# Two heads of attention in the two halves of TensorE's rows, and scores in a two-bank and a one-bank slot

## The chip, the cores and the metric

One core of a Trainium2 chip runs the whole program as one launch. The metric is the device time in microseconds (us). Engines: TensorE (PE; its weight loads are listed as PEld), VectorE (DVE), ScalarE (ACT), GpSimd (POOL) and SyncE (SP), which here only issues DMAs.

## What is computed

Two transformer layers over x of 4 x 1024 x 128 in float32. Cut to what matters:

```python
xn = layernorm(x)
x = x + attn0(xn) + fp4_ffn(xn)         # 16 heads of 8, causal over 1024 keys
xn = layernorm(x)
x = x + attn1(xn) + experts(xn)         # keys: a stride-3 convolution, 342 of them

scores = einsum('bhqd,bhkd->bhqk', q, k) * 8 ** -0.5   # masked: key after query
out = einsum('bhqk,bhkd->bhqd', softmax(scores), v)
# experts: 8 experts, the 2 best per row, plus a shared one
```

## The kernel before, in words

The stages follow each other, with a barrier of all engines between them: `first_projection`, `quantised_ffn`, `attention` for layer 0, `between_layers`, `attention` for layer 1, `experts`.

**Operands.** q and k of a head (8 numbers per row) are cut into three bf16 parts, and their products are summed as 48 rows (`PROWS`). `load_operands` (L193) fetches them for a group of 4 heads: `qp[g]` has 99 partitions (`KROWS + PARTS`), the even head of a pair in rows 0 to 47, the odd head in rows 48 to 95, the other 48 rows of each head at zero, and 3 rows for the maxima; `kp[g]` holds both heads of a pair, one under the other, with ones in the last 3 rows. The zeros are written by ScalarE during the FFN (`clear`, L659), and SP waits for them before it loads (L573). A load is 12 DMAs. The groups of layer 1's first batch are loaded by SP during `between_layers` (group 0, L1294), at the start of `attention` (group 1, L941) and after the first maxima (groups 2 and 3, L960).

**A unit** is one batch element and one group of 4 heads; there are 16 in each layer. For a unit PE computes

- *fills* (L1034 to L1051): scores with queries on the partitions, up to 512 columns in one of three PSUM banks (`BANKS`) used in turn. Where the diagonal is crossed, a matmul with the identity adds a mask (L1044). DVE takes the row maximum of each bank (L1153). In layer 0 there are 38 fills per unit, 16 of them leading ones without a mask; in layer 1 there are 17.
- the *tail*: DVE cuts the negated maxima into three bf16 parts (L1165 to L1173), PE turns them (`turn_max`, L1056), DVE copies them (L1180), and SP stores them with one DMA into the last 3 rows of `qp` (L957).
- *pairs* (L1077): two matmuls of 99 rows with keys on the partitions, one for each head, into the two banks of `p_st[half]`; the maxima's rows subtract the maximum. ScalarE takes the exponential (L1129), POOL zeroes what is unseen (L993) in one of a ring of four buffers (`RING`).
- *weighings* (L1096): probabilities times v in f32, four heads in four groups of 32 columns of the array. A unit has 12 in layer 0 and 5 in layer 1.
- `turn_out` (L1065): the sums, copied by ScalarE (L1138), are turned by four f32 transposes into a bank of the same three, and DVE scales them (L1187, L1191). Two per unit.

**What sets the order.** `Geometry.order` (L758) is a planner that runs in Python when the program is built. It simulates the engines with constants (L58) and writes one list, in which fills of unit n+1, turns, pairs and weighings of unit n are interleaved by readiness and priority. Every engine walks through this list in order. A fill, `turn_max` and `turn_out` each take the next bank; `fresh_bank` (L1028) waits for the use three before.

**Other users.** In layer 0 POOL also cuts the expert weights (L925). In layer 1 it sends rows to the experts' slots (L1005). In `between_layers` SP stores the parts of q and k chunk by chunk (`store_q1`, `store_k1`), and ScalarE waits for the store of a chunk before it overwrites the buffer two chunks later (L1429). In `experts`, DVE casts the first rows (`stage_x`, L1906, called at L1988) before PE's first matmul (L1735), and POOL adds the bias `bo` (L1714) at the start.

## Time and profile before

| | us |
|---|---|
| median of 3 runs | 1249.71 (1248.92 to 1250.62) |
| profiled execution, its own time | 1255.12 |
| its span, first to last instruction | 1253.2 |
| first projection and FFN | to 188.7 |
| attention, layer 0 | 188.7 to about 675 |
| between the layers | to 778.9 |
| attention, layer 1 | 778.9 to 1014 |
| experts | from 1016.8 |

The profile is of one execution. Busy time of PE has modelled ends: matmuls overlap, so its steady rate is better read from starts than from durations. In a timeline merged instructions show as xN with the time from the first start to the last end. Idle time before a group is given with the event that ended it.

### The profile page before, as it was taken

The page shows a single profiled execution, that of the slowest core. Times are in us where ns is not written, and L with a number is a line of the kernel's source. Part 1 is how long each engine was busy: PE and PEld are TensorE (multiplying, and loading weights), DVE is VectorE, ACT ScalarE, POOL GpSimd, SP SyncE. Part 2 cuts the span into 40 slices and gives each one's busy share as a digit, 9 for nine tenths or more (in the row PEclk, how much of TensorE's full clock was granted, in tenths as well). Part 3 has the DMA queues.
Part 4 walks back from the last instruction along what each step waited for, and adds up shares of the span by engine and source line. Part 5 has one row for each costly group of instructions (what it writes and reads, how often), then busy time and mean ns, then how long its engine had stood idle before and what let it go on. Part 6 is the DMA issues. An engine that isn't in the chain of part 4 may idle for free. (4 is left out here: it accounts for less than half of the span.)

```text
span 1253.2 us, 22218 instructions
## 1 busy us (share of the span) xinstructions
PE 1124.7 (90%) x7518; PEld 617.1 (49%) x7518; DVE 943.8 (75%) x2098; ACT 736.4 (59%) x1148; POOL 448.7 (36%) x714
## 2 busy tenths in 40 slices
PE   4668878999999999999998785799998969999997
PEld 2336662343434444444442563344444438888874
DVE  7979979788888888888881563677776646777776
ACT  3567540666666666666667343366666647777762
POOL 6002220232323323322222110366676661566640
PEclk9888996999999999999999796699999989999999
DMA  4322790013202121211000022222222252677543
GB/s 135 101 76 68 112 118 18 2 37 110 85 27 87 53 92 43 87 51 62 27 1 2 9 72 68 61 65 57 65 65 54 72 176 92 188 243 244 175 112 90
DMA packets 94975, 103.52 MB, mean 83 GB/s; under 512 B 17217, under 2 KB 72838, under 8 KB 94864
## 3 DMA queue, kind: packets, MB, share of 16 engines
q1 hardware_dynamic: 88928, 93.09, 27.6%
q0 software_dynamic: 4992, 8.48, 2.0%
q8 instruction: 61, 1.00, 0.3%
q10 hardware_dynamic: 944, 0.54, 0.2%
q14 instruction: 50, 0.41, 0.1%
HBM read 64.67 MB, written 38.43 MB: 82 GB/s over the span
## 5 line engine op out<-in xcount | busy, mean ns | idle before, releaser
L1129 ACT ACTIVATE a_probs<-a_pst 128x1024 f32<-128x1024 f32 (+4 forms) x544 | 413.8, 812 | 283.9 <-PE a_pst L1077 282.5
L1153 DVE TENSOR_REDUCE a_tops<-a_ps 128x1 f32<-128x512 f32 (+9 forms) x624 | 342.3, 591 | 95.0 <-PE a_ps L1047 80.9
L993 POOL TENSOR_SCALAR_AFFINE_SELECT a_probs<-a_probs 128x256 f32<-128x256 f32 (+3 forms) x384 | 180.4, 482 | 386.5 <-ACT a_probs L1129 382.1
L1047 PE MATMUL a_ps<-kp,qp 96*128 96x512 bf16 (+9 forms) x1280 | 293.1, 307 | 0.8 <-DVE a_tops L1153 0.6
L1077 PE MATMUL a_pst<-qp,kp 99*128 99x512 bf16 (+4 forms) x1088 | 259.5, 331 | 14.3 <-DMA qp<-a_top_rows 10.5
L1096 PE MATMUL a_po<-a_probs,vh 128*32 128x512 f32 (+4 forms) x2176 | 231.9, 499 | 2.6 <-POOL a_probs L993 2.5
L1153 DVE TENSOR_REDUCE a_tops_lead<-a_ps 128x1 f32<-128x512 f32 x256 | 161.8, 683 | 5.7 <-PE a_ps L1047 5.5
L1044 PE MATMUL a_ps<-mask_s,identb 128*128 128x128 bf16 (+8 forms) x624 | 144.5, 234 | 13.3 <-DMA kp<-k_parts 6.0
L1047 PEld LDWEIGHTS a_ps<-kp,qp 96*128 96x128 bf16 x1280 | 112.0, 101 | 79.1 <-DVE a_tops_lead L1153 15.4
L1077 PEld LDWEIGHTS a_pst<-qp,kp 99*128 99x128 bf16 (+1 forms) x1088 | 91.8, 99 | 110.1 <-ACT a_probs L1129 43.5
L1044 PEld LDWEIGHTS a_ps<-mask_s,identb 128*128 128x128 bf16 x624 | 59.5, 99 | 132.6 <-DVE a_tops L1153 62.1
L1722 POOL DMA_INDIRECT chosen_rows<-e_slot_y,e_slot_x x92 | 92.8, 1009 | 85.6 <-DVE e_slot_y L1944 43.8
L1932 DVE TENSOR_TENSOR e_tails<-e_hidden,e_heads 128x512 fp32r<-128x512 f32 x124 | 87.1, 703 | 33.1 <-ACT e_heads L1866 29.4
L1096 PEld LDWEIGHTS a_po<-a_probs,vh 128*32 128x32 f32 (+1 forms) x2176 | 43.3, 108 | 71.3 <-issue 61.5
L1859 ACT ACTIVATE e_hidden<-e_pup,e_slot_b 128x512 f32<-128x512 f32 x92 | 63.2, 688 | 24.1 <-PE e_pup L1737 19.2
L1005 POOL DMA_INDIRECT slot_rows<-rows,slots x64 | 63.3, 990 | 14.0 <-issue 11.5
L151 POOL TENSOR_TENSOR f_hq<-f_v,f_sc 128x704 f32<-128x704 f32 x16 | 22.8, 1424 | 119.6 <-DVE f_v L711 112.1
L1187 DVE RECIPROCAL a_inv_sum<-a_ps 128x16 f32<-128x16 f32 x64 | 16.4, 256 | 62.2 <-PE a_ps L1065 58.9
L1065 PE MATMUL a_ps<-ident,a_o_raw 128*128 128x128 f32 x256 | 41.5, 285 | 3.5 <-ACT a_o_raw L1138 1.9
L1138 ACT ACTIVATE a_o_raw<-a_po 128x512 f32<-128x512 f32 x64 | 38.3, 598 | 10.3 <-PE a_po L1096 10.3
L1930 DVE CAST e_heads<-e_hidden 128x512 fp32r<-128x512 f32 x62 | 27.8, 448 | 20.2 <-ACT e_hidden L1859 14.0
L597 PE MATMUL f_pg<-wg,big 128*128 128x352 f32 x64 | 27.4, 512 | 16.9 <-DVE f_h L692 15.9
(294 smaller groups left out, 1636.9 us busy)
## 6 DMA issues: line engine op xcount, KB each, us to landing
e_slot_w<-weight_parts SPq DMA_DIRECT2D x23, 1024.0 KB
weight_parts<-a_cut SPq DMA_DIRECT2D x18, 512.0 KB, 3.0
qp<-q_parts SPq DMA_DIRECT2D x64, 96.0 KB
slot_rows<-empty_row SPq DMA_DIRECT2D x4, 1495.0 KB, 28.6
e_slot_x<-slot_rows SPq DMA_DIRECT2D x23, 260.0 KB
a_raw<-in_wraw SPq DMA_DIRECT2D x18, 256.0 KB, 3.6
qp<-q_parts SPq DMA_DIRECT2D x64, 64.0 KB
q_parts<-o SPq DMA_DIRECT2D x24, 128.0 KB
```

The costliest lines, as they stand in the source:

```text
L993: pool.affine_select(out=seen, in_=seen, compare_op=ALU.is_ge, fill=0.0, base=m0, pattern=[[0, 2], [1, mw]], channel_multiplier=-1 if laye ...
L1005: pool.indirect_dma_start(dram["slots"], bass.IndirectOffsetOnAxis(sb["slots"][:, choice, t:t + 1], 0), sb["rows"][:, t, :], None, bounds_ ...
L1044: pe.matmul(out, sb["identb"][:, :], mask_s[r][:, 0:mw].unsqueeze(1).broadcast_to([P, nh, mw]), start=True, stop=False, skip_group_check=True)
L1047: last = pe.matmul(bank[:, i * room:i * room + w], sb["qp"][slot][0:KROWS, j, f["qt"] * P:(f["qt"] + 1) * P], sb["kp"][slot][0:KROWS, j // ...
L1065: last = pe.transpose(turned[:, t * P:(t + 1) * P], o_raw[:, t * P:(t + 1) * P], sb["ident"][:, :])
L1077: last = pe.matmul(p_st[half][0:st["rows"], i, off:CHUNK], sb["kp"][slot][0:KROWS + PARTS, half, st["kt"] * P:st["kt"] * P + st["rows"]], ...
L1096: last = pe.matmul(p_o[VW * j:VW * (j + 1), st["off"]:CHUNK], sb["vh"][n % 2][0:st["rows"], st["kt"], j, :], probs[local % RING][0:st["row ...
L1129: act.activation(probs[local % RING][0:st["rows"], 2 * part:2 * part + 2, st["off"]:CHUNK], p_st[part][0:st["rows"], :, st["off"]:CHUNK], ...
L1153: dve.tensor_reduce(out, scores, AX.X, ALU.max).then_inc(s["banks_read"], 1)
L1722: pool.indirect_dma_start(dram["chosen"], bass.IndirectOffsetOnAxis(slot_x[r % XR][:, t, E:E + 1].bitcast(U32), 0), slot_y[r % YR][:, t, : ...
L1859: act.activation(hidden[m % RR][:, :], p_up[m % UR][:, :], ACT.Gelu, bias=biases(j)[:, k:k + 1])\
L1932: dve.tensor_tensor(tails[m % HR][:, :], hidden[m % RR][:, :], heads[m % HR][:, :].bitcast(F32), ALU.subtract)\
```

## The change

Each head of a pair gets its own half of the 128 rows: the even head rows 0 to 47 and the maxima's parts rows 48 to 50, the odd head rows 64 to 111 and 112 to 114. `qp` becomes 128 x 2 pairs x T, so nothing has to be cleared. A *couple* is a fill of both heads of a pair (or of both pairs, up to 256 columns). Scores go to a slot of two banks (both heads at once) and a slot of one bank in turn; a couple whose turn is the one-bank slot is done in two halves, one head at a time. The planner's prices change with it (`TWO_AT_ONCE`).

```diff
-KROWS = 2 * PROWS
+ROWS_HALF = P // 2
-BANKS = 3
+SLOTS_OF_BANKS = 2
+BOTH, TWO_AT_ONCE = 2, 1.25
-def load_operands(sp, sb, dram, layer, keys, b, g):
+def load_operands(sp, sb, dram, layer, keys, b, g, halves=range(2)):
-    for odd in range(2):
-        r0 = PROWS * odd
+    for odd in halves:
+        r0 = ROWS_HALF * odd
-            sp.dma_start(sb["qp"][g][rows, odd:GH:2, 0:T], src).then_inc(loaded, 16)
+            sp.dma_start(sb["qp"][g][rows, :, 0:T], src).then_inc(loaded, 16)
...
-        p_s = [... psum_tensor(f"a{layer}_ps{i}", [P, 512], F32) for i in range(BANKS)]
+        p_s = [... psum_tensor(f"a{layer}_ps{i}", [P, 2 - i, 512], F32) for i in range(SLOTS_OF_BANKS)]
```

In the planner's loop, where a fill is taken:

```diff
+                if opened is not None and (mine or taken == C):
+                    f, which, opened = opened, 1, None
+                elif mine:
+                    f, which, opened, taken = taken, 0, taken, taken + 1
+                else:
+                    f, which, taken = taken, BOTH, taken + 1
+                pe = start + ((TWO_AT_ONCE if which == BOTH else 1) * (each_pe[f] + mask_pe[f]))
```

PE's fill. The mask takes two matmuls for each head, since a half of the rows holds only half of the identity (`swapped` is a copy of the constants with the halves exchanged, made by two DMAs):

```diff
+                odds = ((0, 0), (1, 1)) if part == BOTH else ((part, 0),)
                 if f["mask"]:
-                    pe.matmul(out, sb["identb"][:, :], mask_s[r][:, 0:mw]..., start=True, stop=False)
+                    for i in range(2):
+                        for odd, where in odds:
+                            rows = slice(ROWS_HALF * odd, ROWS_HALF * (odd + 1))
+                            pe.matmul(out, sb["idents"][i][rows, :], masks[i][r][rows, 0:mw]..., start=i == 0, stop=False)
-                for i, j in enumerate(f["heads"]):
-                    last = pe.matmul(bank[:, i * room:i * room + w], qp[0:KROWS, j, ...], kp[0:KROWS, j // 2, ...])
+                for i, a in enumerate(f["pairs"]):
+                    for odd, where in odds:
+                        rows = slice(ROWS_HALF * odd, ROWS_HALF * odd + PROWS)
+                        last = pe.matmul(banks[:, where, i * room:i * room + w], qp[rows, a, ...], kp[rows, a, ...])
```

Pairs and maxima:

```diff
                 for i in range(2):
+                    rows = slice(ROWS_HALF * i, ROWS_HALF * i + PROWS + PARTS)
-                                     kp[0:KROWS + PARTS, half, ...], qp[0:KROWS + PARTS, 2 * half + i, ...]
+                                     kp[rows, half, ...], qp[rows, half, ...]
...
-                    sp.dma_start(sb["qp"][n % GROUPS][KROWS:KROWS + PARTS, :, :]..., top_rows[:, :])
+                    for odd in range(2):
+                        r0 = ROWS_HALF * odd + PROWS
+                        sp.dma_start(sb["qp"][n % GROUPS][r0:r0 + PARTS, :, :]..., top_rows[odd * each:(odd + 1) * each, :])
```

DVE reduces both banks of a couple with one instruction. The rest moves work: the eight `clear` passes and SP's waits for them go; in `between_layers` the loads of groups 0 and 1 are issued in four halves of 6 DMAs, one each after the stores of chunks 3, 4, 5 and 6 (before: all 12 of group 0 after chunk 3, group 1 in the next stage); POOL adds the bias in units 1 to 8 of layer 1's attention; DVE stages the first rows of the experts in unit 8:

```diff
+                if what == "end" and layer == 1 and k == 0 and 1 <= n <= CHUNKS:
+                    add_bias(n - 1)
...
+                if what == "end" and layer == 1 and k == 0 and n == B * GROUPS // 2:
+                    stage_first_rows()
...
-            stage_x(0)
             run(step)
```

The memsets of ones in `kp` cover all 128 partitions (before: 3), and PE waits once, at the start of layer 0's attention, for the constants' copies and the experts' empty rows.

## Rows read from the trace of the kernel before

**Rows 1.** The page, busy time of the engines over the span.
```profile
PE 1124.7 (90%) x7518; PEld 617.1 (49%) x7518; DVE 943.8 (75%) x2098; ACT 736.4 (59%) x1148; POOL 448.7 (36%) x714
```
**Rows 2.** Busy time by stretch: first unit, steady part of layer 0, of layer 1.
```profile
core 0: us, PE busy (x) PEld busy (x) DVE busy (x) ACT busy (x) POOL busy (x), PEclk, DMA share, GB/s
188.70:217.00 28.30, 25.37 (x94) 8.15 (x94) 27.39 (x53) 1.28 (x1) 0.73 (x2) 0.63 0.03 8
217.00:660.00 443.00, 440.18 (x3272) 179.20 (x3273) 371.93 (x704) 282.12 (x385) 132.12 (x286) 0.99 0.17 55
...
820.00:990.00 170.00, 158.64 (x1492) 78.64 (x1492) 127.14 (x324) 105.73 (x151) 115.90 (x178) 1.00 0.24 60
```
**Rows 3.** Groups by form, of 260 to 600 us, then of 830 to 980 us.
```profile
L1153 DVE TENSOR_REDUCE a_tops_lead<-a_ps 128x1 f32<-128x512 f32 x185 | 117.0, 683 | 3.3 <-PE a_ps L1047 3.0
...
L1138 ACT ACTIVATE a_o_raw<-a_po 128x512 f32<-128x512 f32 x22 | 13.0, 593 | 0.0
```
**Rows 4.** Timeline, PE: start us, us, engine line op out<-in xcount.
```profile
655.16 0.60 PE L1077 MATMUL a_pst<-qp,kp 99*128 99x512 bf16 x2
655.59 0.38 PE L1047 MATMUL a_ps<-kp,qp 96*128 96x512 bf16 x1
655.90 1.07 PE L1096 MATMUL a_po<-a_probs,vh 128*32 128x512 f32 x8
656.90 0.23 PE L1044 MATMUL a_ps<-mask_s,identb 128*128 128x128 bf16 x1
661.30 0.40 PE L1077 MATMUL a_pst<-qp,kp 99*128 99x128 bf16 x4
745.36 1.03 PE L1326 MATMUL b_pq<-big,wq 128*128 128x512 f32 x2
1002.88 0.66 PE L1065 MATMUL a_ps<-ident,a_o_raw 128*128 128x128 f32 x4
```
**Rows 5.** Timeline, DVE, in the first unit of layer 0.
```profile
195.45 0.68 DVE L1153 TENSOR_REDUCE a_tops_lead<-a_ps 128x1 f32<-128x512 f32 x1
198.46 2.48 DVE L1153 TENSOR_REDUCE a_tops_lead<-a_ps 128x1 f32<-128x512 f32 x4
204.44 1.94 DVE L1153 TENSOR_REDUCE a_tops<-a_ps 128x1 f32<-128x384 f32 x4
```
**Rows 6.** The maxima's store: durations in ns; waits of 260 to 600, of 830 to 980.
```profile
L957 SPq DMA_DIRECT2D qp<-a_top_rows x32: 723/748/794, 214.2 to 996.5; - x32
...
PEld a_pst L1077 <- DMA qp<-a_top_rows: 4.5, 11, 0.6
...
PEld a_pst L1077 <- DMA qp<-a_top_rows: 7.4, 11, 0.7
```
**Rows 7.** Timeline between the layers and at the start of layer 1's attention.
```profile
745.16 0.78 SPq L201 DMA_DIRECT2D qp<-q_parts  x1
...
753.87 7.30 SPq L190 DMA_DIRECT2D q_parts<-q_kept  x6
...
758.26 0.60 ACT L1430 ACTIVATE q_kept<-b_pq 128x512 bf16<-128x512 f32 x1 [12.15 <-DMA q_parts<-q_kept]
...
792.63 0.33 PE L1044 MATMUL a_ps<-mask_s,identb 128*128 128x172 bf16 x1 [5.97 <-DMA kp<-k_parts]
```
**Rows 8.** Start of the experts: timeline; by line, min/median/max ns, first and last start.
```profile
1018.34 1.63 DVE L1914 TENSOR_TENSOR e_xt<-big,e_xh 128x512 fp32r<-128x512 f32 x1
...
L1912 DVE CAST e_xh<-big x8: 419/421/1533, 1016.8 to 1219.5; 128x512 fp32r<-128x512 f32 x8
...
L1716 POOL TENSOR_TENSOR x<-x,bo x8: 1261/1448/1726, 1016.8 to 1026.6; 128x512 f32<-128x512 f32 x8
```
**Rows 9.** FFN: the clearing; busy times with it (92:124) and without (124:156).
```profile
L660 ACT ACTIVATE qp<-identb 96x2048 bf16<-96x2048 bf16 x8 | 15.2, 1901 | 0.0
...
92.00:124.00 32.00, 25.74 (x125) 19.29 (x126) 30.72 (x54) 23.25 (x41) 6.94 (x5) 0.89 0.22 62
124.00:156.00 32.00, 26.79 (x148) 20.66 (x148) 30.72 (x55) 18.65 (x48) 8.32 (x6) 1.00 0.74 112
```

More of the change, by code:

```diff
@@ L727, in __init__ @@
         self.key_tiles = -(-self.keys // P)
-        self.fills, self.steps = [], []
+        self.couples, self.steps = [], []
         for qt in range(T // P):
@@ L732, in __init__ @@
                 if lead:
-                    for j in range(GH):
-                        self.fills.append(dict(heads=[j], qt=qt, k0=0, width=CHUNK, mask=None, partial=True))
+                    for a in range(GH // 2):
+                        self.couples.append(dict(pairs=[a], qt=qt, k0=0, width=CHUNK, mask=None, partial=True))
                 mask_w, mask_r = P, 0
@@ L738, in __init__ @@
                 mask_w, mask_r = width - P * qt // STRIDE, P * qt % STRIDE
-            per = 4 if width <= 128 else 2 if width <= 256 else 1
-            for j in range(0, GH, per):
-                self.fills.append(dict(heads=list(range(j, j + per)), qt=qt, k0=lead, width=width,
-                                       mask=(mask_r, mask_w), partial=False))
+            per = 2 if width <= 256 else 1
+            for a in range(0, GH // 2, per):
+                self.couples.append(dict(pairs=list(range(a, a + per)), qt=qt, k0=lead, width=width,
+                                         mask=(mask_r, mask_w), partial=False))
         for c in range(T // CHUNK):
@@ L769, in order @@
         steps_share = share([2 * p + w for p, w in zip(pair_pe, weigh_pe)])
-        fills_share = share(fill_dve)
         order, pe, dve, act, pool, use = [], 0, 0, 0, 0, 0
-        banks, score_banks, exp_end = [0] * BANKS, [0, 0], {}
+        slot, slots, held, score_banks, exp_end = 0, [0] * SLOTS_OF_BANKS, [None] * SLOTS_OF_BANKS, [0, 0], {}
         split_end, maxima_end, sums_end, copied_end, loaded = {}, {}, {}, {}, dict.fromkeys(range(GROUPS), 0)
-        pairs = fills = sums = 0
+        pairs = sums = filled = taken = halves = 0
+        opened = None
         turns, outs, emptied, sums_free, before = [], [], [], 0, None
@@ L778, in order @@
             at = n + steps_share[k]
-            bank = max(pe, banks[use % BANKS] + PASS_US)
+            bank = max(pe, slots[slot] + PASS_US)
             ready = []
@@ L790, in order @@
                               + (0 if before == "weigh" else PASS_US), 4, "weigh"))
-            m, f = fills // F, fills % F
-            if m < units and m in loaded and m < n + 2 and not (turns and f == F - 1) and (m < 2 or m - 2 in split_end):
-                behind = m + fills_share[f] < at + 1 + AHEAD[self.layer]
+            m = filled
+            if m < units and m in loaded and m < n + 2 and not (turns and halves >= 2 * C - 2) \
+                    and (m < 2 or m - 2 in split_end):
+                behind = m + halves / (2 * C) < at + 1 + AHEAD[self.layer]
                 ready.append((max(bank, loaded[m]), 2 if behind else 5, "fill"))
@@ L945, in _ @@
             use = 0
-            for what, n, k, part in order:
+            for what, n, k, part, slot, before in order:
                 if what == "end" and layer == 0 and n < (B - 1) * GROUPS:
@@ L1027, in _, with fresh_bank @@
         def _(pe):
-            def fresh_bank(use):
-                if use >= BANKS:
-                    pe.wait_ge(s["banks_read"], read(use - BANKS))
-                return p_s[use % BANKS]
-            def fill(n, k, use):
-                f, slot = geo.fills[k], n % GROUPS
-                if k == 0:
-                    pe.wait_ge(sb["loaded"][slot], 16 * LOADS * (layer * B + n // GROUPS + 1))
-                bank, w, nh = fresh_bank(use), f["width"], len(f["heads"])
+            def fresh_bank(slot, before):
+                if before is not None:
+                    pe.wait_ge(s["banks_read"], read(before))
+                return p_s[slot]
@@ L1039, in fill @@
+            def fill(n, k, part, slot, before):
+                f, at = geo.couples[k], n % GROUPS
+                if n // GROUPS not in started[at]:
+                    started[at].add(n // GROUPS)
+                    pe.wait_ge(sb["loaded"][at], 16 * LOADS * (layer * B + n // GROUPS + 1))
+                banks, w, nh = fresh_bank(slot, before), f["width"], len(f["pairs"])
                 room = 512 // nh
+                odds = ((0, 0), (1, 1)) if part == BOTH else ((part, 0),)
                 if f["mask"]:
@@ new lines, in fill @@
+                for i, a in enumerate(f["pairs"]):
+                    for odd, where in odds:
+                        rows = slice(ROWS_HALF * odd, ROWS_HALF * odd + PROWS)
+                        last = pe.matmul(banks[:, where, i * room:i * room + w],
+                                         sb["qp"][at][rows, a, f["qt"] * P:(f["qt"] + 1) * P],
+                                         sb["kp"][at][rows, a, f["k0"]:f["k0"] + w],
+                                         start=not f["mask"], stop=True, skip_group_check=True)
@@ L1100, in weigh @@
                 last.then_inc(s["pv_done"], 1)
-            use = 0
-            for what, n, k, part in order:
+            started = [set() for _ in range(GROUPS)]
+            if layer == 0:
+                pe.wait_ge(sb["later_in"], 16 * (sb["later_loads"] + 4))
+            for what, n, k, part, slot, before in order:
                 if what == "fill":
-                    fill(n, k, use)
+                    fill(n, k, part, slot, before)
                 if what == "pair":
@@ L1118, in _ @@
             use, last_out = 0, None
-            for what, n, k, part in order:
+            for what, n, k, part, slot, before in order:
                 if what == "turn_out":
@@ L1283, in _ @@
         def _(sp):
+            halves = iter([(g, odd) for g in range(2) for odd in range(2)])
             for b in range(B):
```

244 lines of the change are left out of this document (131 added, 113 removed).

## The prediction

> **What bounds the kernel now.** I read the page's busy times first: TensorE (PE) is busy for 90% of the span and VectorE (DVE) for 75% [rows 1]. The stretches come next [rows 2]. In attention 0's steady part (217 to 660 us) PE is busy 440.2 of 443 us at a granted clock of 0.99, DVE 371.9, ScalarE 282.1; in attention 1 (820 to 990) PE 158.6 of 170 us at 1.00, DVE 127.1, ScalarE 105.7, POOL 115.9. So both stages hang on PE. A busy PE includes modelled ends, so I turn to the rate. By the groups of 260 to 600 us, 185 leading reductions (16 for each unit of 4 heads) are 11.56 units, 29.4 us each; in 830 to 980 us, 22 copies of the sums (2 per unit) are 11 units, 13.6 us each [rows 3].
>
> **What a piece costs on PE** [rows 4]. Two bf16 matmuls of 512 columns take 0.60 us and one 0.38, so a column stream of 512 costs about 0.215 us (2.4 GHz); a 512-column f32 matmul fills 1.03 us alone, and a weighing, four of them in four column groups, 1.07. Less the 0.22 us in which the last drains, 0.85. The fill at 655.59 is followed by the weighing 0.31 us later, 0.1 over its stream, and the next work (656.90) comes 1.00 us after that, 0.15 over: a change between forms costs 0.10 to 0.15 us.
> A unit of attention 0 then streams: fills 18432 columns, 7.68 us; masks 4096, 1.71; pairs 18432, 7.68; weighings 4608 columns at four passes, 7.68; turns of the sums, 8 at 0.11 (0.66 less 0.22 for four, the row at 1002.88), 0.88. Sum 25.6; the other 3.8 of 29.4 us are changes of form and waits. Attention 1, with 43 to 342 keys and some 0.05 us as the least for a short matmul (four of 128 columns take 0.40): fills 2.85, masks 1.06, pairs 3.2, weighings 3.2, turns 0.88: 11.2 of 13.6, other 2.4.
>
> **What a piece costs on DVE** [rows 5]. Four reductions of 512 take 2.48 us and one 0.68: one per 0.60, so 0.533 of data and 0.065 fixed; four of 384 take 1.94, one per 0.46, the same fixed part. A unit of attention 0 reads 18432 columns, 19.2 us, in 38 reductions, 2.5, and spends some 2.7 on the split, the turned maxima and the scaling: 24.4, 83% of 29.4. DVE is the next bound.
>
> **The change, part by part.**
> *Pairs.* The two heads sit in rows 0 to 63 and 64 to 127 and write different banks. The trace has no two row groups at once. Bounds: together they take from 1.0 of one (as the four column groups, [rows 4]) to 2.0 (serial). I take 1.1, since the column groups are the nearest row. Attention 0: 7.68 becomes 4.22; attention 1: 3.2 becomes 1.76.
> *Fills.* Slots alternate, and three turns per unit take one too, so two couples of three go whole into the two-bank slot and the third as two halves through the one-bank slot, with no partner. The factor is 2/3 x 0.55 + 1/3 = 0.70: 7.68 becomes 5.38, and 2.85 becomes 2.0.
> *Masks.* Half the rows carry half the identity, so each head's mask takes two matmuls. Whole couples stream as much as before x 1.1, halves double: 1.71 becomes 2.39. In attention 1 there are 40 short ones for 17 at about 0.05 us: 1.06 becomes 1.9.
> PE's streams, attention 0: 25.6 becomes 20.6. Attention 1: 11.2 becomes 9.7.
> *Maxima in two stores.* SP issues a second DMA, 0.75 us each now [rows 6]; PE's first pair waits for the last and has the fills queued behind it. That store already ends eleven idle times of the weight loads in 260 to 600 us (4.5 us in all) and eleven in 830 to 980 (7.4), so it is not covered. The second should land 0.6 us later (0 to 0.8): +0.6 per unit, and SP's next loads slip as much.
> *Form changes.* Turns of maxima and sums were in the same full form as the fills and no longer are: 3 per unit, some 0.1 each way: +0.3 (0 to 0.6).
> PE then needs 20.6+3.8+0.9 = 25.3 us per unit, and 9.7+2.4+0.9 = 13.0.
> *DVE.* 27 reductions for 38: 24.4 becomes 23.6; attention 1 (13 for 17) 10.2 becomes 9.9.
> *The slots.* Three banks let PE run 1.2 us ahead of DVE; two slots only one read, 1.13 us or 0.60 in turn. While a half is read for 0.60 us PE must fill two banks, about 0.5 us to the reduction (mask 0.11, stream 0.215, drain some 0.2, [rows 4]), and a weighing of 1.0 us in between leaves DVE empty. PE at 25.3 and DVE at 23.6 could run at 25.3 or, if the pairs cost 1.0, at 24.6; I estimate 1.4 us lost per unit (0 to 3.3): 26.7. In attention 1, PE 13.0, DVE 9.9: +0.2, 13.2.
> Attention 0: 15 steady units x (29.4-26.7) = -40 us. Attention 1: 15 x 0.4 = -6. First units only fill, at half clock (0.63 in 188.7 to 217, [rows 2]): two banks take 0.4 longer there, +1 us per stage, +2 together.
> *Loads in halves* [rows 7]. From 745.16 SP issues 12 loads until 753.87; the store of the next chunk's q stands behind them, and ScalarE waits 12.15 us for it. Six go first now: -4.3 at this wait, the next store is 3 earlier: -3 (0 to -4.5) at the stage's end. Chunk 7's store stands behind the last half, but attention 1's barrier is later.
> *Group 1 loaded early.* Attention 1's second unit waits 5.97 us for its operands, issued only behind chunk 7's stores: -6 (-4 to -6.5).
> *Early staging* [rows 8]. The cast (from 1016.8) and the remainder (to 1019.97) of the first rows stand before the first expert matmul: -3.2. They move to DVE in unit 8, 1.1 us, where it has slack. The bias goes to POOL in units 1 to 8, 1.45 each, queued before POOL's zeroing that weighings wait for; POOL has 54 us free in 170 and the ring of four covers it. POOL's adds no longer run beside DVE's first steps (cast 1.53 us against a median 0.42): about -1.8. Together -5.
> *Clearing gone.* Eight passes of 1.90 us leave ScalarE, but DVE is busy 30.72 of 32 us with them and without [rows 9]: 0. Loads and empty rows start earlier in a stage that waits for neither; memsets of kp cover more partitions but as many elements in each: 0 (they end long before kp is loaded). The two copies of the constants are small.
> Sum: -40-6+2-3-6-5 = -58. The profiled execution took 1255.1 us (span 1253.2), 5.4 over the median 1249.7; I take the difference from the median: **1192**.
>
> By the Trainium skill's "TensorE: Matmul & The Clock Gate", Part 3 (Packing small matmuls), four row tiles were measured at 3.07 times one, not 4; an estimate of 1.3 for two follows. No row here shows row groups. With 1.3 in place of 1.1, by the same sum, PE needs 1.5 us more per unit of attention 0 and 0.5 of attention 1, and the time would be some 1220.
>
> **Rivals.**
> *A: the row groups do not run at once.* Pairs and fills stay, all masks double. Attention 0 +1.7+0.9 = 2.6 a unit, attention 1 +1.3+0.9 = 2.2: +72-12 = 1310 us. Against it: column groups overlap fully. 5%.
> *B, slower: the clock.* PE streams 25.6/29.4 = 87% now at full clock, 20.6/26.7 = 77% then. The granted clock did fall in the first unit, where PE only fills for DVE [rows 2]. At half clock a unit costs 41.2+4.7 = 45.9 in attention 0 (+19) and 19.4+3.3 = 22.7 in attention 1 (+10): 435 us for all. It decides above 58/435 = 13% of the steady stretch; at 20% the time is 1279. For it: two heads at once leave PE idle. Against: in 124 to 156 us it stays 1.00 with PE busy 26.8 of 32, less by streams [rows 9]. 7%.
> *C: the slots cost more.* DVE empties behind each weighing: 28.6 and 13.8 per unit, -12+3, and -12 elsewhere: 1229. For: weighings of 1 us against reads of 0.6. 19%.
> *D: DVE is kept fed.* With pairs at 1.0 of one, 24.6 and 12.2: -72-21-12: 1145. For: the planner orders the work by these slots. 12%.
> Forecast 57%.
>
> **How the numbers follow.** About 0.2% can be told from no change. The forecast's own range is 1165 to 1218. Faster: forecast, C and D, less 2% of C's upper end for no change, 86%; same 2%; slower A and B, 12%. The range for 8 in 10 leaves out A and B above and half of D below, 18% in all: 1147 to 1240.
>
> **What would show it.** Right: the two pair matmuls of 512 in under 0.45 us; units at 26 to 27.5 and 12.7 to 13.7 us; DVE over 88% in attention 0 with reductions of 1024 at 1.2 us; 27 reductions per unit; the wait on the maxima 0.6 longer; no 12 us wait near 750, no 6 us wait in attention 1, the first expert matmul with the stage's start. Wrong: pair matmuls one after the other (A), a clock under 0.9 in the steady parts (B), DVE under 84% with waits on fills behind weighings (C).

## The result and the profile after

The changed kernel takes 1349.16 us in the median of 4 runs (1339.30 to 1351.88), where the kernel before took 1250.16 beside it: a ratio of 1.078 (1.072 to 1.084), slower by 7.8%. The prediction was 1192 us, in a range of 1147 to 1240, and gave "slower" a chance of 0.12. Both the sign and the range were wrong.

The profiled execution took 1339.3 us, its span is 1337.4. On the page TensorE is busy for less of a longer span [rows 1], and its clock, which was 0.99 and 1.00 in the steady parts of the kernel before [rows 2], is at 7 or 8 tenths in both attentions (at 5 and 6 where they start):
```profile
PE 1123.7 (84%) x8295; PEld 573.0 (43%) x8302; DVE 950.5 (71%) x1873; ACT 727.2 (54%) x1140; POOL 447.5 (33%) x714
...
PE   4658877888888888888897786878889889999997
...
PEclk9979985888877788888888896877877878999999
```
Now by stage. All stages below are cut at the first score matmul and the last turned sum. Busy times of the kernel before, attention 0 and attention 1 (columns as in [rows 2]):
```profile
188.80:691.60 502.80, 491.61 (x3568) 195.18 (x3568) 402.45 (x766) 304.61 (x417) 140.98 (x308) 0.97 0.15 49
778.90:1013.30 234.40, 212.07 (x1888) 102.37 (x1888) 162.19 (x414) 136.86 (x193) 148.17 (x228) 0.95 0.24 62
```
The same stages of the changed kernel, and two stretches inside attention 0, one after the other:
```profile
core 0: us, PE busy (x) PEld busy (x) DVE busy (x) ACT busy (x) POOL busy (x), PEclk, DMA share, GB/s
189.10:743.70 554.60, 477.29 (x3984) 163.22 (x3984) 399.38 (x591) 308.74 (x417) 141.95 (x308) 0.83 0.14 44
824.40:1102.60 278.20, 230.73 (x2256) 93.78 (x2256) 178.62 (x366) 137.19 (x193) 157.41 (x236) 0.78 0.19 51
...
551.80:562.00 10.20, 9.69 (x55) 3.59 (x57) 5.91 (x9) 4.02 (x5) 2.03 (x5) 0.50 0.23 66
562.00:585.90 23.90, 20.08 (x200) 6.90 (x196) 19.76 (x28) 15.19 (x21) 8.47 (x16) 1.00 0.22 73
```
Attention 0 is 51.8 us longer and attention 1 43.8; the start takes 0.3 more, and the rest is shorter: between the two 80.7 us for 87.3, from attention 1's end to the first expert matmul 3.6 for 6.8, the experts 231.2 for 233.1. That is the whole difference of the spans (1337.4 against 1253.2). The clock does not sink a little; it swings between its two levels, here 10 us at 1.2 GHz and 24 at 2.4, and the swing has the length of a unit (33.4 us on average; 6.8 to 13.7 us of each are at 1.2 GHz).

The timeline of the changed kernel shows what went as planned, and where a unit ends:
```profile
547.60 0.19 DVE L1196 TENSOR_TENSOR a_tops<-a_tops,a_tops_lead 128x16 f32<-128x16 f32 x1
...
548.44 1.30 POOL L940 TENSOR_TENSOR first_rows<-a_raw,first_rows 128x512 fp32r<-128x512 f32 x1
548.65 1.13 DVE L1205 CAST a_top_parts<-a_top_rest 128x32 bf16<-128x32 f32 x1
...
550.05 1.54 DVE L1186 TENSOR_REDUCE a_tops<-a_ps 128x2 f32<-128x256 f32 x2
550.61 0.23 PE L1081 MATMUL a_ps<-consts,a_top_parts 128*96 128x128 bf16 x1 [2.02 <-DVE a_tops L1186]
551.52 0.21 DVE L1214 COPY a_top_rows<-a_ps 96x128 bf16<-96x128 bf16 x1
551.74 1.05 PE L1090 MATMUL a_ps<-ident,a_o_raw 128*128 128x128 f32 x4 [0.90 <-DVE a_top_rows L1214]
...
565.71 0.41 PE L1103 MATMUL a_pst<-qp,kp 51*128 51x512 bf16 x2
...
566.86 0.38 PE L1103 MATMUL a_pst<-qp,kp 51*128 51x512 bf16 x2
```
At the full clock two pair matmuls of 512 columns now take 0.38 to 0.41 us, as one did, where the two took 0.60 [rows 4]. Rival A is out. At the unit's end PE stands still for 2.02 and 0.90 us. The turn of the maxima has to wait for a slot, and that slot's fill is read by a reduction which stands on DVE behind the five steps of the split; one of these, the cast, takes 1.13 us beside a POOL addition (0.18 where POOL does nothing). Then come the copy, the two stores (1.5 us of issue) and only then the next pairs. In the kernel before the planner left 2 to 2.5 steps of pairs to be done when the split began, with 8 or 9 pieces of work between the turn and the next unit's first pair; by the changed costs and slots it leaves 1 step and 4 pieces (the orders of the two kernels' planners, attention 0).

### The profile page after: what moved, and what is told of

It is laid out like the page before. It is cut to its first block and busy times, and to the rows that moved or that the text cites. A ratio compares the mean times of both kernels' runs of the same rounds, so it can differ in the third digit from the quotient of the medians.

```text
span 1337.4 us, 23579 instructions
## 1 busy us (share of the span) xinstructions
PE 1123.7 (84%) x8295; PEld 573.0 (43%) x8302; DVE 950.5 (71%) x1873; ACT 727.2 (54%) x1140; POOL 447.5 (33%) x714
## 5 line engine op out<-in xcount | busy, mean ns | idle before, releaser
L1186 DVE TENSOR_REDUCE a_tops<-a_ps 128x2 f32<-128x86 f32 (+14 forms) x466 | 331.6, 740 | 114.2 <-PE a_ps L1072 112.2
L1103 PE MATMUL a_pst<-qp,kp 51*128 51x512 bf16 (+4 forms) x1088 | 233.2, 386 | 37.4 <-DMA qp<-a_top_rows 25.1
L1072 PE MATMUL a_ps<-kp,qp 48*128 48x512 bf16 (+9 forms) x1280 | 250.0, 346 | 3.0 <-DVE a_tops L1186 2.7
L1186 DVE TENSOR_REDUCE a_tops_lead<-a_ps 128x1 f32<-128x512 f32 (+1 forms) x189 | 159.9, 872 | 42.6 <-PE a_ps L1072 41.8
L1066 PE MATMUL a_ps<-consts 64*128 64x256 bf16 (+4 forms) x704 | 116.0, 246 | 32.1 <-DVE a_tops L1186 15.6
L1066 PEld LDWEIGHTS a_ps<-consts 64*128 64x128 bf16 x704 | 48.0, 100 | 181.9 <-DVE a_tops L1186 94.8
L1103 PEld LDWEIGHTS a_pst<-qp,kp 51*128 51x128 bf16 (+1 forms) x1088 | 68.7, 102 | 122.4 <-ACT a_probs L1155 63.6
L1072 PEld LDWEIGHTS a_ps<-kp,qp 48*128 48x128 bf16 x1280 | 87.0, 108 | 77.1 <-DVE a_tops_lead L1186 45.1
L1066 PE MATMUL a_ps<-swapped 64*128 64x256 bf16 (+4 forms) x704 | 115.5, 245 | 0.0
L153 POOL TENSOR_TENSOR f_hq<-f_v,f_sc 128x704 f32<-128x704 f32 x16 | 22.7, 1421 | 119.4 <-DVE f_v L709 117.7
L1090 PE MATMUL a_ps<-ident,a_o_raw 128*128 128x128 f32 x256 | 47.6, 316 | 14.2 <-DVE a_top_rows L1214 11.5
L1066 PEld LDWEIGHTS a_ps<-swapped 64*128 64x128 bf16 x704 | 51.7, 107 | 14.5 <-issue 9.3
```

The lines of the kernel that those rows point to most:

```text
L1066: pe.matmul(out, sb["idents"][i][rows, :], masks[i][r][rows, 0:mw].unsqueeze(1).broadcast_to([ROWS_HALF, nh, mw]), start=i == 0, stop=Fals ...
L1072: last = pe.matmul(banks[:, where, i * room:i * room + w], sb["qp"][at][rows, a, f["qt"] * P:(f["qt"] + 1) * P], sb["kp"][at][rows, a, f[" ...
L1103: last = pe.matmul(p_st[half][0:st["rows"], i, off:CHUNK], sb["kp"][at][rows, half, st["kt"] * P:st["kt"] * P + st["rows"]], sb["qp"][at][ ...
L1186: dve.tensor_reduce(out, scores, AX.X, ALU.max).then_inc(s["banks_read"], 1)
```

## The experiments

A unit is timed from one turn of the maxima to the next. In the medians, each kernel is compared with runs of the kernel before on the same chip (1250.8 to 1251.6 us).

**The planner's constants.**
```diff
-    0.00042, 0.105, 0.07, 0.00104, 0.165, 0.17, 0.00083, 1.1, 2.2, 9.0)
+    0.00042, 0.105, 0.07, 0.00104, 0.165, 0.17, 0.00083, 3.0, 3.6, 9.0)
```


> The changed kernel with two constants of its planner set nearer to what its own trace shows: the split of the maxima 3.0 us for 1.1, their store 3.6 for 2.2. Nothing else differs but the order of the same work. Theory M (the chain of the maxima: the last fill of a unit, the split, the turn and the two stores stand between a unit's last pair and the next one's first, since the planner now leaves one step of pairs behind the split where it left 2 to 2.5 before; TensorE runs dry there and the clock falls because of it): with three steps left the wait of TensorE for the split maxima, 3.1 us per unit of attention 0, falls under 1, units of attention 0 go from 33.5 to 28 to 30 us, the granted clock there from 0.85 to over 0.93, and the time to 1250 to 1290 us. Theory K (the clock falls because two heads at once leave TensorE with less to stream, wherever the gaps lie): the clock stays under 0.88 and the time within 1 per cent of 1349. Theory S (two slots starve VectorE at each fill): units stay over 32 us.


1343.8 us, 1.074 (1.072 to 1.076). Busy times of e1, attention 0:
```profile
189.80:736.20 546.40, 493.97 (x3984) 171.10 (x3984) 393.43 (x590) 308.11 (x417) 141.86 (x308) 0.83 0.14 45
```
The gaps went: the stretch from the turn at 415.5 to that at 446.8 us has none over 0.6 us. Yet the clock is at 0.83 as before, and attention 0 gained 8 us. So the clock does not need the gaps; theory M as the sole cause fell here. Not one unit is free of half clock: those with 6.8 us of it take 31.2 to 31.9 us, those with 20.5 take 36.7.

**Filler where TensorE waits for the split.**
```diff
+                spare = fresh_bank(slot, before)
+                for _ in range(10):
+                    pe.matmul(spare[:, 0, :], sb["identb"][:, :], sb["kp"][n % GROUPS][:, 0, 0:CHUNK], start=True, stop=True)
                 pe.wait_ge(s["split_steps"], ...)
```


> The changed kernel with ten extra matmuls of 512 columns into the free slot before TensorE waits for the split maxima of a unit (their result is overwritten), 2.2 us of streams at full clock in a gap of 3.1. Theory K: the granted clock rises from 0.85 to over 0.93 in attention 0 and, since the units took 31.6 us in the stretches at full clock against 33.5 over all, the time falls by 20 to 35 us, to some 1320. Theory M: the clock may rise, but the chain stays: units stay over 31 us and the time within 1.5 per cent of 1349. If the clock stays where it is, the gap behind the turned maxima (their stores) is enough by itself to lower it.


1401.5 us, 1.117 (1.110 to 1.124). Attention 0 of e2:
```profile
189.00:769.90 580.90, 499.80 (x4144) 172.55 (x4144) 400.57 (x591) 307.51 (x417) 142.44 (x308) 0.88 0.13 42
```
Neither expectation was met. The filler needs the slot as well, so it ran behind the wait and not in it (a gap of 1.9 us stands ahead of it still), and it lengthened the chain. What it did show: ten full-height matmuls more in each unit, and the clock of attention 0 at 0.88 for 0.83, although the unit grew. More work and more height go together here, so this run does not tell them apart.

**Three slots of one bank again.**
```diff
-SLOTS_OF_BANKS = 2
+SLOTS_OF_BANKS = 3
...
+                    pe.matmul(out, sb["identb"][:, :], masks[0][r][:, 0:mw]..., start=True, stop=False, ...)
+                for i, (odd, a) in enumerate(f["heads"]):
+                    rows = slice(ROWS_HALF * odd, ROWS_HALF * odd + PROWS)
```


> The changed kernel with the scores in three slots of one bank again and the order of work, the masks and one head per bank as before; the pairs keep the two heads in two halves of the rows. Two reductions more in a unit of attention 0 and three more in attention 1 than before. Theory S: VectorE is fed as before, units of attention 0 fall to 26 to 28 us and of attention 1 to 13.3, time 1190 to 1230. Theory M: the planner leaves 1.5 steps behind the split (2 to 2.5 before, 1 in the changed kernel), so the wait for the maxima is in part still there: units 29 to 31, time 1250 to 1300. Theory K: TensorE has the least to stream of all versions, the clock stays under 0.88 and the time over 1300.


1407.1 us, 1.125 (1.122 to 1.127), slower than the changed kernel. Of the three expectations only theory K's (a clock under 0.88, over 1300 us) fits. TensorE's timeline in e3 shows a cause that none of them names:
```profile
405.18 0.23 PE L1053 MATMUL a_ps<-consts 128*128 128x128 bf16 x1
405.34 0.33 PE L1057 MATMUL a_ps<-kp,qp 48*128 48x384 bf16 x1
405.61 0.23 PE L1053 MATMUL a_ps<-consts 128*128 128x128 bf16 x1
405.77 0.33 PE L1057 MATMUL a_ps<-kp,qp 48*128 48x384 bf16 x1
```
The same in the kernel before:
```profile
657.19 0.22 PE L1044 MATMUL a_ps<-mask_s,identb 128*128 128x128 bf16 x1
657.25 0.38 PE L1047 MATMUL a_ps<-kp,qp 96*128 96x512 bf16 x1
```
A mask of 128 columns is followed by its fill after 0.16 us when the fill is in half height, after 0.06 when both are full: 0.10 us for the change. Back to full height costs as much (384 columns stream in 0.16, the next mask comes 0.27 later). Two units of e3 that stand one after the other:
```profile
454.90:492.50 37.60, 36.46 (x230) 10.65 (x227) 26.37 (x52) 19.55 (x26) 9.48 (x20) 0.77 0.14 50
492.50:524.00 31.50, 30.59 (x229) 9.76 (x225) 25.57 (x50) 19.24 (x26) 7.87 (x19) 0.95 0.15 43
```
The work is the same and TensorE has next to no gap in either; the clock alone makes 6.1 us. By these two, 1 us at half clock costs an estimated 0.45 us, and a unit wholly at 2.4 GHz would take some 30 (0.95 is 3.4 us at half clock: 31.5 less 1.5).

**Masks in halves too, three slots.**
```diff
-                    pe.matmul(out, sb["identb"][:, :], masks[0][r][:, 0:mw]...)
+                    for i in range(2):
+                        pe.matmul(out, sb["idents"][i][rows, :], masks[i][r][rows, 0:mw]..., start=i == 0, ...)
```


> The kernel of e3_one_bank (three slots of one bank, two heads of a pair in two halves of the rows) with the masks in halves of the rows too, as in the changed kernel: two matmuls of 64 rows for each. In e3_one_bank the units of attention 0 took 31.6 us with 3.4 us at half clock and 37.5 with 17.1, a line with 0.43 us per us at half clock and 30.2 at none. Theory F (a change between full height and half height costs TensorE 0.09 to 0.11 us: mask to fill 0.178 us there against 0.085 in the kernel before): with 40 changes per unit less and 1.7 us of masks more the line falls to 27 to 28.5 us at none, and the time to 1330 to 1370, since the clock still falls. Theory S (the two slots are what slows the changed kernel at full clock): the line falls below 27, and the time below 1300. If neither form nor slots matter it stays at 1407.


1288.8 us, 1.030 (1.028 to 1.033). Both stages of e5:
```profile
188.60:713.30 524.70, 472.75 (x3984) 170.34 (x3984) 413.46 (x798) 307.04 (x417) 142.42 (x308) 0.85 0.14 47
794.80:1056.90 262.10, 217.20 (x2256) 94.68 (x2256) 182.93 (x464) 135.19 (x193) 157.56 (x236) 0.84 0.19 54
```
118 us less than e3, with one edit, which takes out some 40 changes of height per unit: they were dear (theory F), though the time is below F's range and in S's. It is also 60 us under the changed kernel, which differs from it in slots and order alone, so theory S has its part, though at a low clock one cannot say how much of this the slots cost by themselves (e13 below can).

**Less for TensorE, all of it in full height.** The kernel of before without one of each pair's two matmuls from the second unit on; what it computes is then not the reference's.
```diff
-                for i in range(2):
+                for i in range(1 if n else 2):
```


> The kernel of before, all matmuls in full height and three slots, which leaves out the second head's matmul of each pair from the second unit of each attention on: its scores are whatever the bank held, and the output is not the reference's. TensorE streams 3.84 us less per unit of attention 0, 21.8 us; the other engines do the same work. Theory K (the granted clock follows how much TensorE streams): units cannot go under VectorE's 24.4, TensorE's share of streams falls from 87 to 80 per cent or less and the clock falls in part of each unit, so that units stay at 27 to 30 us in place of 26 to 26.5. Theory R (row halves or the gaps at the unit's ends lower the clock, and full-height work does not): the clock stays 1.0, units are 26 to 27 us and the time 1180 to 1200.


1214.6 us, 0.971 (0.968 to 0.974). Twelve units of attention 0 in e6:
```profile
275.20:608.10 332.90, 322.22 (x2368) 118.30 (x2369) 298.91 (x575) 225.26 (x310) 108.06 (x232) 1.00 0.21 69
```
The clock never left 2.4 GHz there, with streams of 21.8 in 27.7 us (79%, about the share that the prediction gave the changed kernel) and gaps of up to 1.5 us at the units' ends. Theory K, that such a share is enough to lower the clock, fell; the time, 1214.6, is above theory R's range. For taking 3.84 us of streams out of a unit shortened it by 1.9 (from 29.6 over the same twelve units), not by 3.8, in a kernel with nothing else changed. Waits of the weight loads (us in total, times, longest) over twelve units of the kernel before, then of e6:
```profile
PEld a_pst L1077 <- ACT a_probs L1129: 18.4, 51, 0.8
...
PEld a_pst L1077 <- ACT a_probs L1129: 32.9, 78, 0.8
```
The waits for ScalarE's exponentials grow by 1.2 us per unit; those of the fills' weight loads for DVE's reductions by 2.1 (53.6 to 78.4 us), with DVE busy for 298.9 of 332.9 us.

**The pair matmuls twice, in half height.**
```diff
-                for i in range(2):
+                for i in (0, 1, 0, 1):
```


> The changed kernel with each pair's two matmuls issued twice in turn (the same result again): TensorE streams 3.84 us more per unit of attention 0, as much as before the change, in half heights. Theory K by streams: the clock returns to over 0.95 in attention 0, units (33.3 us on average with 10.2 us at half clock, about 29 at full) take 31 to 33 us, and the time is no more than 1 per cent above 1349 or below it. Theory R (half-height work or gaps lower the clock): the clock stays at 0.85 to 0.88 and units grow by 3 to 5 us, the time to 1410 or more.


1395.1 us, 1.116 (1.113 to 1.119). Attention 0 of e7:
```profile
190.00:787.90 597.90, 539.21 (x4752) 209.73 (x4752) 401.61 (x591) 310.93 (x417) 142.10 (x308) 0.82 0.13 41
```
3.84 us of half-height streams more in each unit, and the clock stays down: theory R held in the clock, with the gaps of the changed kernel in place (its time is 15 us under R's range). The units grew to 36 us, so that streams are still a smaller share of them than in e6; this run alone does not rule the share out. With e1 (gaps gone, clock low) and e6 (gaps there, clock full) it points to the height of the matmuls, which the next run tests alone.

**All 64 rows of a half.** The rows added hold zeros on one side, so the columns and the result stay. Outside the attentions ScalarE zeroes `qp` again during the FFN, and each load has two small transfers more.
```diff
-                    rows = slice(ROWS_HALF * odd, ROWS_HALF * odd + PROWS)
+                    rows = slice(ROWS_HALF * odd, ROWS_HALF * (odd + 1))
...
+        sp.dma_start(sb["qp"][g][r0 + PROWS:r0 + PROWS + PARTS, :, :]..., sb["zeros"][...]).then_inc(loaded, 16)
```


> The kernel of e5_half_masks whose fills and pairs run over all 64 rows of their half in place of 48 and 51; the rows added hold zeros on one side (the rows of the maxima are zeroed with each load, two small transfers more), so the result is the same and the columns streamed are the same. Theory H (the granted clock falls because the array is used in less of its height: 48 or 51 rows of a half now, 96 and 99 of 128 before, while full-height work at 78 per cent of the time in e6_less_pairs kept 1.0): the clock of attention 0 rises from 0.87 to 0.9 or more, units from 31.4 to 29 to 30.5 us, the time from 1289 to 1255 to 1275. Theory G (rows do not matter; halves at once simply leave TensorE idle more often, or the gaps at the units' ends lower the clock): nothing changes, 1285 to 1295.


1274.5 us, 1.021 (1.018 to 1.025). Both stages of e8:
```profile
188.20:694.50 506.30, 457.08 (x3984) 168.01 (x3984) 413.52 (x798) 307.81 (x417) 141.92 (x308) 0.88 0.15 49
778.50:1035.80 257.30, 204.13 (x2256) 91.64 (x2256) 184.52 (x464) 135.34 (x193) 157.07 (x236) 0.90 0.21 56
```
Multiplying by zeros made the kernel 14 us faster than e5. In the profiled executions (e5's is its slowest, e8's its fastest) attention 0 took 506.3 for 524.7 at 0.88 for 0.85, attention 1 257.3 for 262.1 at 0.90 for 0.84. In the steady stretch from 260 to 660 us the clock is 0.90 for 0.87, and a unit takes 30.3 us for 31.4: theory H, at the upper end of its time. Theory G is out. The transfers of zeros are not free: the stage between the layers takes 84.0 us for 81.5.

**Padded, with the planner's constants.** e8 with the edit of e1.

> e8_padded with the planner's constants of e1_plan (split of the maxima 3.0 us, store 3.6), which leaves 2 to 2.5 steps of pairs behind the split for 1.5. In e5_half_masks TensorE is idle 2.96 us per unit of attention 0, 1.8 of it before the turned maxima in most units. Theory M: that gap goes, units 1 to 2 us shorter than in e8_padded, the time 15 to 35 us shorter. If the clock rules all, units stay as in e8_padded and the time within 8 us of it.


1274.8 us, 1.019 (1.017 to 1.021), no gain on e8 in the sum, but not in the stages:
```profile
190.10:681.40 491.30, 449.62 (x3984) 165.79 (x3984) 398.29 (x798) 305.34 (x417) 142.92 (x308) 0.96 0.15 51
765.40:1036.80 271.40, 219.47 (x2256) 93.78 (x2256) 172.78 (x464) 138.02 (x193) 158.01 (x236) 0.86 0.19 53
```
In attention 0 padding and a filled end of the unit together hold the clock: thirteen of the fourteen units after the first two run wholly at 2.4 GHz and take 29.0 to 29.5 us; the stage is 11.5 us shorter than before the change. Attention 1 lost 14 us by the same constants.

**Pairs alone in halves (e9), and no halves at all (e11), both with the planner's constants of e1.** e9 keeps three slots and puts fills and masks back in full height (its pairs have 51 rows, not 64):
```diff
-                    rows = slice(ROWS_HALF * odd, ROWS_HALF * odd + PROWS)
+                    rows = slice(0, ROWS_HALF + PROWS)
```


> Pairs alone in two halves of the rows; fills over rows 0 to 111 (the other head's rows zero) and masks in full height, three slots of one bank, up to four heads in one, the other parts of the change kept, planner constants as in e1_plan. TensorE streams 3.84 us less per unit of attention 0 than e4_rest, and changes height at 20 to 35 places per unit for 0.1 us each. Theory F: the changes take 2 to 3.8 us back, units 28.5 to 30 us at full clock; theory H: with fills and masks in full height the clock is over 0.95. Together 1215 to 1240 us, against 1237 for e4_rest. If the clock falls below 0.92 here too, a half-height part of 3.8 us per unit is enough for it, and the time is 1240 to 1280.

e11 is e4 (below: all in full height, the other parts of the change kept) with the edit of e1.

> e4_rest (the kernel of before with the other parts of the change) with the planner's constants of e1_plan. Before, TensorE hardly waits at a unit's end (0.17 us idle per unit of attention 0, 0.9 of attention 1), so little is to be had: 1228 to 1240 us against 1237 for e4_rest; units of attention 1 that take 13.3 us may fall to 13.0.

e9: 1274.7 us, 1.018 (1.016 to 1.020). e11: 1267.3 us, 1.013 (1.011 to 1.015). Stages of e9:
```profile
188.40:703.30 514.90, 482.51 (x3568) 154.48 (x3568) 393.69 (x767) 306.76 (x417) 142.24 (x308) 0.98 0.15 48
787.60:1039.40 251.80, 218.68 (x1888) 93.19 (x1888) 163.52 (x417) 138.09 (x193) 157.88 (x236) 0.91 0.20 57
```
Stages of e11:
```profile
189.50:700.20 510.70, 495.18 (x3568) 193.05 (x3568) 399.95 (x766) 307.48 (x417) 142.68 (x308) 0.98 0.15 48
783.10:1030.70 247.60, 220.35 (x1888) 104.43 (x1888) 161.33 (x416) 137.94 (x193) 157.47 (x236) 0.95 0.20 57
```
Both missed their ranges, e11 by the constants: against e4 below, it has the same work and 8 us more in attention 0 and 22 in attention 1. That e9 missed for the same reason is argued, since it ran with these constants alone. An order that suits one layout is a bad one for another. At equal constants the steps read: pairs in halves, with the second store of the maxima (e11 to e9), cost 4.2 us in each attention, although they take 61 us of streams off attention 0, and the steady part of attention 0 stays at 2.4 GHz; fills and masks in halves as well, all padded (e9 to e10), gain 23.6 us in attention 0 and cost 19.6 in attention 1.

**The other parts of the change alone.** The kernel of before with the loads in halves, group 1 early, the bias and the first expert rows in attention 1.

> The kernel of before with the other parts of the change alone: attention 1's operands loaded in halves with group 1 early, the bias added and the first expert rows split in attention 1. By the terms of the prediction (3, 6 and 5 us) 1236 us, 1232 to 1242; all theories of attention expect the same, and granted clock 1.0 in both attentions as before. If it is not faster than before, those terms are wrong too.


1237.3 us, 0.989 (0.987 to 0.991), as expected. Stages of e4:
```profile
191.20:694.00 502.80, 490.46 (x3568) 194.85 (x3568) 402.58 (x766) 304.51 (x417) 140.74 (x308) 0.98 0.15 49
774.70:999.90 225.20, 211.40 (x1888) 102.33 (x1888) 161.51 (x416) 136.34 (x193) 158.50 (x236) 0.96 0.23 62
```

**Each attention in the form that suits it.** Attention 0 as in e10, attention 1 in full height as in e4.
```diff
+        tail_us, store_us = (3.0, 3.6) if self.layer == 0 else (TAIL_US, STORE_US)
...
+                    rows = slice(ROWS_HALF * odd, ROWS_HALF * (odd + 1)) if layer == 0 else slice(0, ROWS_HALF + PROWS)
```


> Attention 0 as in e10_padded_plan (two heads in padded halves of the rows, three slots of one bank, the planner's split 3.0 and store 3.6 us), attention 1 as in e4_rest (everything in full height, one store of the maxima, the old constants), the other parts of the change kept; what stays extra in attention 1 are the two small transfers of zeros with each load. Attention 0 took 491.3 us in e10_padded_plan against 502.8 in e4_rest, attention 1 225.2 in e4_rest: if the stages add up, the time is 1237 less 11, 1223 to 1230, below both kernels. If the stages do not add up (the clock of one stage carried into the next, the transfers of zeros in the way of loads) it is 1232 or more.


1229.2 us, 0.982 (0.981 to 0.984), below both kernels of this case. Stages of e12:
```profile
189.00:681.10 492.10, 450.82 (x3984) 165.92 (x3984) 397.30 (x798) 305.30 (x417) 142.36 (x308) 0.95 0.16 51
765.10:992.90 227.80, 211.60 (x1888) 101.80 (x1888) 161.43 (x416) 136.27 (x193) 158.24 (x236) 0.96 0.24 63
```
The stages add up within 3.4 us; attention 1's extra is small, and after its first fills and the unit behind them it runs at 2.4 GHz throughout, as before the change. Packing, in attention 0 alone and with new constants, gives some 8 us (1229.2 for e4's 1237.3).

**The changed kernel with both repairs**: the edits of e1 and e8 in it, its two slots kept.

> The changed kernel, two slots of two banks and one, with the two repairs that brought the three-slot version to 1275: all 64 rows of each half in fills and pairs, and the planner's split 3.0 and store 3.6 us. Theory H+M (height and the planner's constants are what the changed kernel lacks; the slots cost little): attention 0 goes from 554.6 us to 495 to 505 with the clock over 0.95, the time to 1270 to 1290. Theory S (the two slots cost 1 to 3 us per unit at full clock by themselves): units of attention 0 take 30.5 to 32 us where e10_padded_plan's took 29.0 to 29.2, TensorE and VectorE wait for one another in turn, the clock falls again in a part of each unit, and the time is 1295 to 1330.


1290.0 us, 1.031 (1.027 to 1.036). Both stages of e13:
```profile
190.70:696.10 505.40, 447.05 (x3984) 160.57 (x3984) 389.49 (x590) 305.70 (x417) 141.51 (x308) 0.94 0.15 49
780.70:1052.20 271.50, 214.58 (x2256) 89.16 (x2256) 175.59 (x366) 139.16 (x193) 157.59 (x236) 0.86 0.20 53
```
Units wholly at 2.4 GHz take 29.4 to 29.5 us, those of e10 mostly 29.0: two slots cost some 0.5 us per unit by themselves. Four of e13's units fell to half clock for a while, one of e10's did. So theory H+M holds for most of it, just past the slow end of its ranges for the stage and the clock.
Beside e1 this is the sharpest test of the height, for only the padding differs: the same slots, planner's constants and columns, and the same longest gap in a unit (0.6 us). The time falls by 54 us, attention 0 from 546.4 to 505.4 and its clock rises from 0.83 to 0.94; in e1 every unit is at half clock for a part, in e13 ten of fourteen for none. Those ten stream 20.6 us by the prediction's count in 29.4, a share of 70%, less than e6's 79, and hold 2.4 GHz. In attention 1 the two repairs together gain 6.7 us (278.2 to 271.5), and the clock stays at 0.86.

## Why the prediction was wrong

**The step that failed is the weight of rival B.** The prediction set the clock's fall at 7% and costed it at 1279. It named both sides: TensorE would stream less of the time, and in the stretch of 124 to 156 us the clock stays full with PE busy for less [rows 9]. The second argument decided, and it compared busy time alone; that stretch has six gaps, of 0.9 us at most, and matmuls of 96 and 128 rows. What the sum left out is that half-height matmuls do not hold the clock here as full-height ones do. With 48 and 51 rows in each half no unit of e1 stays at 2.4 GHz, with 64 in each half most of e13's do, with the same columns in the same order; e5 to e8 says the same with three slots. Nor does the share of streams by itself lower the clock, as the argument for rival B had it: 79% in e6 and 70% in e13's units hold it.
The decision point was right as far as it went. In the steady parts of the changed kernel the clock is 0.85 (248 to 683 us) and 0.80 (851 to 1085 us), so that 31 and 40% of them are at half clock, both far over 13%. With these shares and rival B's own units (26.7 and 45.9; 13.2 and 22.7) a unit comes to 31 and 15.9 us; measured are 33.4 and 16.7. By the prediction's sum that is an estimated 1297 us: the clock accounts for some 105 of the 157 us that the prediction missed. The rest is below.

**The unit at full clock was too short, 26.7 against 29.4 (e13).** The sum took every microsecond of streams saved as a microsecond gained, down to DVE's 24. e6 gives the measured exchange: 3.84 us fewer streams, 1.9 us shorter units, with more waits for ScalarE and for DVE. By this exchange the 5.0 us of streams saved (25.6 to 20.6) would have given an estimated 2.5. With the sum's own 0.9 for stores and changes and the slots' measured 0.5 (below) that is a unit of 28.3; the last 1.1 us of the 29.4 stays open. The terms beside it:
- Pairs at 1.1 of one: 1.0 in the trace, better than taken. The same holds for two fills of 512 in two halves (0.39 us for both).
- A change of form at 0.1 us: right (e3). In e9 units take 30.8 us, as in e11: some 25 new changes per unit between pairs and fills by the planner's order, an estimated 2.5 us, take most of the 3.84.
- Two slots at 1.4 us (0 to 3.3): 0.5 at full clock (e13 against e10). In the changed kernel, with the planner's constants and clock as they are, slots and order cost 60 us (e5). Rival C's mechanism, DVE left without a fill, is there in part (it waits for fills 6.5 us per unit, 2.5 before); the dearer place was the turn of the maxima, which waits for a slot whose fill is read behind the split. The prediction did not look there. Rival D had the pairs right at 1.0, but no packed version kept DVE fed: in e13's units at full clock it is busy for 83%.
- The second store at 0.6 us: PE's weight loads wait for the maxima's transfers 11.0 us in 12 units of attention 0, 0.9 each, where it was 0.4 [rows 6]: right. In attention 1 PE itself waits for them 14.7 us over 15 units for 6.7, and 4.5 of it are one wait (to 873.4), where both stores stand in SP's queue behind the loads of another group.
- That the planner would keep the units' ends covered was not weighed at all. It plans with a split of 1.1 us and a store of 2.2, which did no harm while the fills ran 2 steps ahead.

**Attention 1 at 13.2 us was wrong even at full clock.** Units of the changed kernel without half clock take 14.8 to 16.0. Masks of two short matmuls for each head and two stores put pieces with a fixed cost where the streams are short; the fills and masks are the larger part (e9 to e10, 19.6 us, some of it clock: 0.91 to 0.86). How the rest divides, and what keeps the clock low there when the rows are padded (0.86 in e13), stays open.

**The other parts were right.** In e4 the first expert matmul comes 3.6 us after the last turned sum for 6.8, the experts take 231.2 for 233.1: 5.1 us, 5 predicted. The stage between gains 6.6 (3 predicted) and attention 1 9.2 (6 predicted for group 1 alone); by the medians 13.6 in all against 14. (The stages add up to more, 18.5, because the profiled execution of the kernel before is 5 us over its median.) The longest wait before ScalarE's `q_kept` fell from 12.15 to 7.6 us, by some 4.5, and where attention 1's second unit waited 5.97 us for group 1's operands [rows 7] no wait of PE itself for a load is over 0.7:
```profile
ACT q_kept L1477 <- DMA q_parts<-q_kept: 17.5, 5, 7.6
```
(Waits of the changed kernel: us in total, times, longest.)

By the Trainium skill's "TensorE: Matmul & The Clock Gate", Part 1 (The HAM clock gate), the clock follows how busy TensorE has been lately. The traces agree that it swings between two levels, but busy time as columns streamed does not tell which: e1 and e13 stream the same columns, at 0.83 and 0.94 in attention 0, and e5 and e8 do, at 0.85 and 0.88.
From the 3.07 times for four row tiles in Part 3 (Packing small matmuls) of the same page of the Trainium skill the prediction had worked out 1.3 for two at once as an alternative; the trace does not agree with this estimate, with 0.38 to 0.41 us for two matmuls of 512 against 0.38 for one.

## What to carry to other kernels

Packing two half-filled matmuls into the array's height frees TensorE's time and at the same time makes its work lighter, and a lighter TensorE can lose its clock before the next bound is reached; count on the gain only where the freed time is really used. If it falls, try filling the rows with zeros: it costs no column, though the zeros have to be loaded or written. When the layout of a pipelined stage changes, its planner's constants and the slack at unit boundaries must be read anew from the trace, stage by stage, since the same packing gained in the stage with long matmuls and lost in the one with short ones. A stage's price per microsecond of the bound engine is best measured by leaving work out, as e6 did: here it was one half.

## What was not expected of the hardware

- Zeros in 16 and 13 more rows per half, with the same columns, took 18 us off a stage of 525 (e5 to e8) and 41 off one of 546 (e1 to e13), with the clock at 0.88 for 0.85 and 0.94 for 0.83.
- The clock can lock to the work: in the changed kernel it falls in every unit of attention 0's steady part, within 4 us of the turn of the maxima, and is back 6.8 to 13.7 us later. In e3 units of the same work take some 31.6, 33.2 or 37.6 us by how long it stays down (3.4, 6.8 or 17.1 us).
- Matmuls of different row halves run at once though they belong to different operations: in e3 a fill of 384 columns and the first pair matmul both start at 405.77.
- A cast of 32 columns on DVE took 1.12 to 1.13 us beside a POOL addition of 1.30 in eight units of attention 0 of the changed kernel, 0.18 in those where POOL does nothing, and it stands in the chain of the maxima.
